# Context, norm and queries of the first layer in one block, with the mask counted instead of kept

## What is computed

```
n = layernorm(x);  q = n @ wq.T + bq;  k = ctx @ wk.T + bk;  v = ctx @ wv.T + bv     (16 heads of 16)
scores = q k^T / 4;  scores = -inf where mask == 0;  a = softmax(scores) v;  y = a @ wo.T + bo
x = x + tanh(g_xattn) * y;  then a gated mixture of experts on layernorm(x)
```

## Time and profile before

| | us |
|---|---|
| median of 3 runs | 1854.36 (1853.82 to 1856.44) |
| the profiled execution | 1838.9 |
| its span, first to last instruction | 1837.2 |
| busy: PE, DVE, ACT, POOL | 1497.6, 1178.2, 860.9, 180.8 |
| mean granted TensorE clock | 0.903 |

### The profile page before, as it was taken

The page is one execution under the profiler, slowest core; times in us unless marked ns, Lnnn a source line. Parts: engine busy times, 40 slices in busy tenths (PEclk is TensorE's granted clock), DMA queues, the critical chain, the costliest instruction groups (busy, mean ns, idle before and its releaser), DMA issues. The chain is left out here.

```text
span 1837.2 us, 23827 instructions
## 1 busy us (share of the span) xinstructions
PE 1497.6 (82%) x7833; PEld 871.9 (47%) x7834; DVE 1178.2 (64%) x2309; ACT 860.9 (47%) x1544; POOL 180.8 (10%) x248
## 2 busy tenths in 40 slices
PE   6564999968997899992399999999999987848870
PEld 3232333347886788882153334333334334735550
DVE  2564999763311677776299999999999935502335
ACT  3121777722111555550217777777777773211110
POOL 3520000000300000003000000000000000061116
PEclk9786999987999999996759999999999998778995
DMA  7935422112101899981723112112111100533114
GB/s 240 373 104 170 119 54 54 28 48 69 46 0 68 321 333 340 343 290 60 217 58 81 43 29 40 23 24 45 24 23 25 23 1 1 125 107 114 43 43 137
DMA packets 108667, 196.87 MB, mean 107 GB/s; under 512 B 8959, under 2 KB 80372, under 8 KB 108568
## 3 DMA queue, kind: packets, MB, share of 16 engines
q1 hardware_dynamic: 101633, 180.71, 31.4%
q0 software_dynamic: 4608, 12.59, 2.2%
q10 hardware_dynamic: 2326, 2.31, 0.4%
HBM read 144.69 MB, written 50.36 MB: 106 GB/s over the span
## 5 line engine op out<-in xcount | busy, mean ns | idle before, releaser
L920 DVE TENSOR_REDUCE attend_piece_max<-attend_p_bank 128x1 f32<-128x400 f32 (+3 forms) x1280 | 669.2, 589 | 68.8 <-PE attend_p_bank L808 56.5
L900 ACT ACTIVATE attend_probs<-attend_s_bank 128x512 f32<-128x512 f32 (+1 forms) x1088 | 565.7, 602 | 244.0 <-PE attend_s_bank L819 244.0
L808 PE MATMUL attend_p_bank<-attend_k_st,attend_q_st 62*128 62x400 f32 (+2 forms) x1280 | 416.6, 435 | 55.3 <-DMA attend_k_st<-ones_rows 50.8
L819 PE MATMUL attend_s_bank<-attend_q_st,attend_k_st 64*128 64x512 f32 (+1 forms) x1088 | 402.4, 448 | 36.6 <-ACT attend_probs L900 21.7
L819 PEld LDWEIGHTS attend_s_bank<-attend_q_st,attend_k_st 64*128 64x128 f32 (+1 forms) x1088 | 172.2, 183 | 359.0 <-ACT attend_probs L900 351.6
L836 PE MATMUL attend_o_bank<-attend_probs,attend_v_st 128*32 128x512 f32 (+1 forms) x2176 | 291.0, 607 | 1.4 <-ACT attend_probs L900 1.4
L808 PEld LDWEIGHTS attend_p_bank<-attend_k_st,attend_q_st 62*128 62x128 f32 x1280 | 209.2, 194 | 104.0 <-issue 52.5
L1530 DVE TENSOR_TENSOR slots_w_low<-slots_w_up,slots_w_high 128x2048 fp32r<-128x2048 f32 x46 | 105.1, 2287 | 45.7 <-ACT slots_w_high L1526 45.7
L1340 DVE TENSOR_TENSOR share_hid<-share_b_bank,share_g_act 128x512 f32<-128x512 f32 (+1 forms) x40 | 27.6, 691 | 116.7 <-PE share_b_bank L1191 105.5
L1526 ACT ACTIVATE slots_w_high<-slots_w_up 128x2048 fp32r<-128x2048 f32 x46 | 87.8, 1910 | 5.8 <-DMA slots_w_up<-in_L_ffn_W_dram 5.6
L1797 POOL DMA_INDIRECT collect_back<-back,keep_f_place x48 | 47.1, 982 | 381.1 <-PEq L1786 367.1
(11 more groups left out here) (234 smaller groups left out, 1810.1 us busy)
## 6 DMA issues: line engine op xcount, KB each, us to landing
slots_w_up<-in_L_ffn_W_dram SPq DMA_DIRECT2D x46, 1024.0 KB, 7.4
slots_w_dn<-in_L_ffn_W_dram SPq DMA_DIRECT2D x23, 1024.0 KB, 5.9
ctx_raw<-in_mask_BxSxS_ik_dram SPq DMA_DIRECT2D x16, 800.5 KB, 8.2
q_rows<-q_part SPq DMA_DIRECT2D x24, 512.0 KB, 4.0
attend_q_st<-q_rows SPq DMA_DIRECT2D x64, 192.0 KB, 4.6
k_rows<-ctx_k_part SPq DMA_DIRECT2D x12, 800.5 KB, 10.0
attend_k_st<-k_rows SPq DMA_DIRECT2D x32, 300.2 KB, 5.8
sorted<-keep_zeros SPq DMA_DIRECT2D x6, 1024.0 KB, 9.7
```

Source lines behind the costliest of these rows:

```text
L808: last = pe.matmul(bank[:, 0:even(kn)], q_st[rows, slot, t * P:(t + 1) * P].bitcast(F32R), k_st[rows, slot, k0:k0 + even(kn)].bitcast(F32R ...
L819: last = pe.matmul(out, k_st[rows, hs, kt * P:kt * P + kn].bitcast(F32R), q_st[rows, hs, q0:q0 + CH].bitcast(F32R), start=True, stop=not m ...
L900: act.activation(probs[0:kn, (kt + hs) % RING, q0:q0 + CH], s_bank[(NC * kt + c + hs) % RING][0:kn, :], ACT.Exp).then_inc(exp_done, 1)
L920: dve.tensor_reduce(dst, bank_of(i, n)[:, 0:kn], AX.X, ALU.max).then_inc(entry_done, 1)
```

## The change

One block, `prepare`, takes the place of `prepare_context`, `normalise` and `project_queries` for the first layer; the second layer keeps the latter two.

- x is loaded ahead of the mask, in four parts; the statistics are taken behind the context's copies, and the norm and the queries come between the first layer's keys and the values. The second layer's keys come last.
- ACT writes keys and queries once, rounded; DVE computes the low part from PSUM, (bank + bias) - rounded, piece by piece. `k_full` and `full` are gone. Keys have a ring of three units, queries a ring of three halves, values a ring of four, PSUM two rings of four and three banks. The query weights are scaled when they are copied.
- The mask tiles have a ring of four. They aren't converted and kept: DVE adds (tile == 0) onto one bf16 tile for 12 of them, with one instruction each, and POOL onto another for 4 (tiles 3, 7, 11, 15), with two. PE's column sums take both. `find_ends` compares counts and not sums of -2^100. In the branch on all keys, the mask is loaded and converted there (`load_mask` as a function).
- `find_ends`, `find_window` and the store of `key_mask` move into the block, and their small operations with them.

The diff, cut to its core:

```diff
--- before.py
+++ after.py
...
-def prepare_context(nc, io, const, scratch, mask_q, unseen, x_now, stats):
+def prepare(nc, io, const, scratch, unseen, x_now, window):
...
-        names = [f"L{l}_xattn_w{w}" for w in order for l in range(2)]
-        NW, WR, LOADS, VR = len(names), 4, 4, 2
+        sc = Scope(nc, ctx, "prep")
+        names = [f"L{l}_xattn_w{w}" for w, l in ("k0", "q0", "v0", "v1", "k1", "q1", "o0", "o1")]
+        NW, WR, LOADS, VR, RR, KR, QR, XR = len(names), 4, 4, 4, 4, 3, 3, 4
...
-        k_full = sc.sb("k_full", [P, DB, S], F32)
-        k_part = sc.sb("k_part", [P, PART, DB, S], F32)
+        q_bias = sc.sb("q_bias", [P, DB], F32)
+        k_part = sc.sb("k_part", [P, KR, PART, S], F32)
+        q_part = sc.sb("q_part", [P, QR, PART, HALF], F32)
...
+        raw = sc.sb("raw", [P, RR, S], I32)
+        masked = [sc.sb(f"masked_{n}", [P, S], BF16) for n in ("dve", "pool")]
...
+        a_bank = [sc.ps(f"a_bank{n}", [P, CH], F32) for n in range(4)]
+        b_bank = [sc.ps(f"b_bank{n}", [P, CH], F32) for n in range(3)]
...
+            for n, t in enumerate(on_pool):
+                pool.wait_ge(landed[t % RR], 16 * (t // RR + 1))
+                pool.wait_ge(counted[1], n + 1)
+                pool.tensor_scalar(flag[:, :], raw[:, t % RR], 0.0, None, ALU.is_equal).then_inc(flagged, 1)
+                pool.wait_ge(flagged, n + 1)
+                pool.tensor_tensor(masked[1][:, :], masked[1][:, :], flag[:, :], ALU.add).then_inc(counted[1], 1)
...
-            load_mask(0)
-            load_mask(1)
-            for n, (l, b) in enumerate(units):
-                for t in range(2 + AHEAD * n, 2 + AHEAD * (n + 1)):
-                    load_mask(t)
...
+            for n in range(2):
+                load_weights(n)
+            for n in range(4):
+                sp.dma_start(x_now[:, 4 * n:4 * n + 4], io["x"][0].rearrange("(t p) d -> p t d", p=P)[:, 4 * n:4 * n + 4])\
+                    .then_inc(x_in[n], 16)
+            for t in range(RR):
+                load_mask(t)
+            for n in range(2, WR):
+                load_weights(n)
+            store_keys(0)
+            load_mask(4)
+            store_keys(1)
+            for t in range(5, 9):
+                load_mask(t)
+            for n in range(4):
+                store_queries(n)
+                load_mask(9 + n)
+            for n in range(WR, NW):
+                load_weights(n)
+            for t in range(13, QT):
+                load_mask(t)
+            for kt in range(KT):
+                store_values(kt)
+            for u in (2, 3):
+                store_keys(u)
...
-            pe.wait_ge(copied, 4)
+            pe.wait_ge(w_copied, 1)
             pe.wait_ge(c_copied, KT)
...
+            for u in range(DB):
+                for c in range(NP):
+                    keys(u, c)
+            for n in range(QT // 2):
+                bank = take(1, b_bank, x_copied, n + 1)
+                for t in (2 * n, 2 * n + 1):
+                    pe.wait_ge(scaled, t + 1)
...
+            pe.wait_ge(w_copied, 2)
+            for n, (b, c) in enumerate(q_tiles):
+                bank = take(0, a_bank, q_low, n + 1)
+                pe.wait_ge(x_copied, 2 * (c + 1))
...
+            for n in range(2, WR):
+                turn_weight(n)
+            pe.wait_ge(w_copied, WR)
             for kt in range(KT):
-                if kt >= 2:
-                    pe.wait_ge(v_added, kt - 1)
+                bank = take(1, b_bank, v_added, kt + 1)
...
-            pe.wait_ge(k_copied, 2 * len(chunks))
-            for n in range(4, NW):
+            for n in range(WR, NW):
...
-            pe.wait_ge(merged, QT)
+            pe.wait_ge(counted[0], len(on_dve) + 1)
+            pe.wait_ge(counted[1], len(on_pool) + 1)
             for kt in range(KT):
                 kn = keys_of(kt)
-                pe.matmul(unseen[0:kn, kt:kt + 1], tile_sum[:, kt * P:kt * P + kn], ones[:, :], start=True, stop=True)
+                for n in range(2):
+                    last = pe.matmul(unseen[0:kn, kt:kt + 1], masked[n][:, kt * P:kt * P + kn], ones[:, :],
+                                     start=(n == 0), stop=(n == 1))
+            last.then_inc(scored, 1)
+            for u in (2, 3):
+                for c in range(NP):
+                    pe.wait_ge(w_copied, WR + 1)
+                    keys(u, c)
...
+            act.wait_ge(stable, 1)
+            act.activation(std[:, :], var[:, :], ACT.Sqrt).then_inc(rooted, 1)
+            for u in range(DB):
+                round_keys(u)
...
+            for n, (b, c) in enumerate(q_tiles):
+                act.wait_ge(q_ready, n + 1)
+                if n // 2 >= QR:
+                    act.wait_ge(q_stored[n // 2 - QR], 16 * PRODUCTS)
+                act.activation(q_part[:, n // 2 % QR, 0, c % 2 * CH:(c % 2 + 1) * CH].bitcast(F32R), a_of("q", n)[:, :],
+                               ACT.Identity, bias=q_bias[:, b:b + 1]).then_inc(q_high, 1)
+            for n in range(2, NW):
                 copy_weight(n)
+            for u in (2, 3):
+                round_keys(u)
...
+            left = list(on_dve)
+
+            def count_masks(n):
+                for t in left[:n]:
+                    dve.wait_ge(landed[t % RR], 16 * (t // RR + 1))
+                    dve.wait_ge(counted[0], on_dve.index(t) + 1)
+                    dve.scalar_tensor_tensor(out=masked[0][:, :], in0=raw[:, t % RR], scalar=0.0, in1=masked[0][:, :],
+                                             op0=ALU.is_equal, op1=ALU.add).then_inc(counted[0], 1)
+                del left[:n]
...
+            def split_keys(u):
+                l, b = units[u]
+                if u >= KR:
+                    dve.wait_ge(k_stored[u - KR], 16 * PRODUCTS)
+                for c, (k0, kn) in enumerate(PIECES):
+                    n = NP * u + c
+                    dve.wait_ge(k_high, n + 1)
+                    dve.scalar_tensor_tensor(out=k_part[:, u % KR, 1, k0:k0 + kn].bitcast(F32R),
+                                             in0=a_of("k", n)[:, 0:kn],
+                                             scalar=const["bqk"][:, (2 * l + 1) * DB + b:(2 * l + 1) * DB + b + 1],
+                                             in1=k_part[:, u % KR, 0, k0:k0 + kn], op0=ALU.add, op1=ALU.subtract)\
+                        .then_inc(k_low, 1)
...
+            for t in range(QT):
+                dve.wait_ge(x_in[t // 4], 16)
+                dve.bn_stats(stats[:, t], x_now[:, t]).then_inc(measured, 1)
...
+            dve.tensor_scalar(var[:, :], mv[:, :, 1], 1e-5, None, ALU.add).then_inc(stable, 1)
+            dve.wait_ge(b_copied, 1)
+            split_keys(0)
+            dve.wait_ge(rooted, 1)
+            dve.reciprocal(inv[:, :], std[:, :]).then_inc(inverted, 1)
+            count_masks(1)
+            split_keys(1)
+            dve.wait_ge(inverted, 1)
+            for t in range(QT):
+                if t >= XR:
+                    dve.wait_ge(x_turned, (t - XR) // 2 + 1)
+                dve.tensor_scalar(x_n[:, t % XR], x_now[:, t], mv[:, t, 0:1], inv[:, t:t + 1], ALU.subtract, ALU.mult)\
+                    .then_inc(scaled, 1)
+            dve.wait_ge(bias_ready, 1)
+            for n, (b, c) in enumerate(q_tiles):
+                dve.wait_ge(q_high, n + 1)
...
+                dve.scalar_tensor_tensor(out=q_part[:, n // 2 % QR, 1, at].bitcast(F32R), in0=a_of("q", n)[:, :],
+                                         scalar=q_bias[:, b:b + 1], in1=q_part[:, n // 2 % QR, 0, at], op0=ALU.add,
+                                         op1=ALU.subtract).then_inc(q_low, 1)
+                if n % 2 == 0:
+                    count_masks(1)
             dve.wait_ge(bv_in, 64)
             for kt in range(KT):
                 kn = keys_of(kt)
                 dve.wait_ge(v_ready, kt + 1)
                 if kt >= VR:
                     dve.wait_ge(v_stored[kt % VR], 16 * (kt // VR))
-                dve.tensor_tensor(v_out[0:kn, kt % VR].rearrange("p l d -> p (l d)"), bank[2 + kt % 2][0:kn, :],
+                dve.tensor_tensor(v_out[0:kn, kt % VR].rearrange("p l d -> p (l d)"), b_of("v", kt)[0:kn, :],
                                   bv[0:kn].rearrange("p l d -> p (l d)"), ALU.add).then_inc(v_added, 1)
-                if AHEAD * len(units) + kt < QT:
-                    convert(AHEAD * len(units) + kt)
-            dve.wait_ge(x_in, 16)
+                count_masks(1)
+            count_masks(len(left))
+            find_ends(dve, unseen, key, score, hidden[:, :], touched[:, :], ends, numbered, scored)
+            split_keys(2)
+            split_keys(3)
+            dve.wait_ge(ends_turned, 1)
+            dve.tensor_copy(hidden_row[:, :], unseen[0:KT, P:2 * P]).then_inc(row_copied, 1)
+            find_window(dve, turned_ends, choice, window, ends_turned, stepped)
...
-    everywhere, anywhere = NEG * (T - 0.5), NEG * 0.5
+    everywhere, anywhere = T - 0.5, 0.5
+    dve.wait_ge(scored, 1)
...
```

(85 more changed lines are left out.)

247 lines of the change are left out of this document (138 added, 109 removed).

## The result

| | changed | before |
|---|---|---|
| median, first comparison (4 runs each) | 1840.8 us (1838.55 to 1842.48) | 1854.09 us (1853.46 to 1856.44) |
| median, second comparison | 1823.99 us | 1842.46 us |
| median, third comparison | 1824.92 us | 1841.76 us |

The ratio of the first is 0.992 (0.9908 to 0.9932): faster by 13.3 us, where 13 had been forecast, with 1841.4 us as the time. The two repeats, on other chips, give 0.9899 (0.9884 to 0.9914) and 0.9913 (0.9897 to 0.9928), 18.5 and 16.8 us. The range, 1826 to 1862 us, was laid around a time before of 1854.36 us and stands for anything from 28 us less to 8 us more; all three differences are inside it.

A forecast was written before the change was run, and what follows sets the result against it. It saw a transfer-bound first part, then a compute-bound second. The new timeline ran to 138 us, plus 4 made 142 against 155: 13 us off the 1854.36 us median, 1841.4 us, range 1826 to 1862.

The forecast's parts named there:

- both waits: ACT about 9 us at about 52 for a query store; DVE about 20 us near 76 for the first value store.
- Start to first keys: Block's start: context's last copy at 21.1, keys start at 23.4, variances at 27.8, first key unit done at 30.8.
- Count, unit 1, norm: After the first keys: count 1.8 us, second key unit done at 35.5, 16 scalings 5.3 us, x copied at 42.
- Queries: After the norm: 1.75 us per tile, six done at 52.5, then a store wait landing at 62; values start at 65.
- Values: After queries: four added at 76, wait to 97, POOL's comparison of 2 to 6 us hidden there, nine tiles to 112.
- Weights, sums, second keys, stores: Block's end: four weights 3.8 us, sums to 117, second layer's keys 11 us to 128, last store landed at 138.
- Borders: Block borders: two vanish, their time already in the difference because ends are compared.
- The lump of 4 us: Added to 138 at the end: DVE two-input operations held once or twice by POOL, and some queries or keys at lower clock.
- B: Rival, chance 0.20: transfers pack better, value stores come sooner, end of the stretch at 128, time 1827 us.
- C: Rival, chance 0.15: gain eaten on DVE, five two-input operations held by POOL cost 14 us; 1855, no change.
- D: Rival, chance 0.15: PE at the lower clock after stalls, 31 us more, end at 169, 1868 us, slower.
- The frame: Change touches only what runs up to 157 us; some 1680 us behind stay, and over 3 us change there disproves it.

The follow-up runs named there:

- the pair on one chip: Changed kernel and kernel before, both without edit, profiled in the third comparison: ratio 0.9913, POOL's first memset of the attention at 145.94 and 158.43 us.
- the earlier trace: Profiled execution of the kernel before, without edit, from which the prediction took its prices: 1838.9 us.
- the experiment without POOL: Changed kernel with all 16 mask tiles counted by DVE and none by POOL: 1817.87 us, ratio 0.9867, memset 136.99.
- two rings: Changed kernel with a fourth half for queries and values 4 to 11 in x_nt's space: 1805.1 us, ratio 0.98, memset 127.11.

## Why the prediction came out right, step by step

The difference was right to 0.3 us in the first comparison and 5.5 and 3.8 us short in the repeats. At the memset, where all 13 us were forecast, it was 11.5 us between the first profiles and 12.5 in the pair on one chip; the rest came from behind it, where nothing was forecast. The path held, as did both waits and their places. But the steps' times were too early nearly throughout, and the 4 us added at the end happened to cover it: the last landing, forecast at 138 and at 142 with them, came at 143.5. That much of the hit is luck.

1. *Start to first keys.* "I take the same time: its last copy ends at 21.1" failed: the context's last copy ended at about 18.0, 3.1 us sooner, and first keys started at 19.6 and not 23.4. Beside x the context comes faster than beside the mask: with x behind four masks the last copy ended at 24.4. x itself came later than the 20 that I had named, DVE waiting for it until 21.3 in this profile. The variances were ready at 25.5 (27.8). The low part is 0.63 us (0.57).
2. *Count, unit 1, norm.* The count alone is 1.77 to 1.82 us, as taken; its mean is 2.17 with the held ones. Unit 1 was done at 34.0 (35.5). "16 scalings of 0.33 us" failed: 10.22 and not 5.3 us, for the two instructions that POOL held. "0.33 us each" was right only without POOL: 5.7 and 5.25 us for all 16 in two runs where POOL is idle then. The forecast had priced POOL's contention only against two-input operations, and put it at the end as a lump. x was copied at 45.3 (42).
3. *Queries.* Eight tiles took 13.9 us at the full clock, 1.74 each, as in the earlier trace rows. The wait was there: until 67.4 (62), 11.8 us long (9). Of these 5.4 us, 3.1 are the store's later issue, at 56.9 (53.8), which follows from x's late copy; the other 2.3 it took longer to land, behind four masks.
4. *Values.* Four were added at 81.3 (76); the wait was 19.4 us (20) and ended at 103.6 (97), with a share of 1.0 to 1.04 from 80 to 100 us. "Between 2 and 6 us it hides in this wait" is the step that failed: POOL's comparison takes 4.27 us, inside its bounds, but it does not hide. Mask 15 could be issued only after it and the addition, 7.5 us in all, and the value stores stood behind mask 15. Behind the wait, nine tiles took 18.1 us and not 15: two counts were held by POOL (3.63 and 4.23), 4.2 us together.
5. *Weights, sums, second keys, stores.* Four weights took 1.91 us, half of the 3.83 of the earlier trace rows, at a granted clock of 1.00 by the profile in both places. The pace casts doubt on that for the early one: this kernel's first weights (8 transposes in 1.97 us at 17.7) go at 0.21 us from one start to the next, much as x's do at a granted clock of 0.50 (30 in 6.22 us, 0.20 each), and the late ones at 0.11. So the price that I took from the earlier trace rows looks like one of the lower level, though no run tested it. The second keys ran from 123.3 to 134.3, 11.0 us as forecast, 6 us late; the six stores were issued from 129.6 to 137.1, and the last landed at about 143.5, two before the memset as in the earlier trace rows. Memset 145.7, against 144.
6. *Borders.* Nothing showed there.
7. *The lump of 4 us.* In kind it was right (DVE held by POOL: 4.9 in step 2, some 4 in step 4), and it was too small.

**Rivals.** B (transfers pack better, memset 130) did not happen, but its reason was sound: freed of the two waits, the kernel does just that. C's mechanism is real and cost about 7 us, not 14, which the experiment without POOL shows; with 7 in place of the 4 added, the forecast would have been 3 us further from what was measured and better in reasoning. D did not happen: second keys and queries ran at 1.00. Its reasoning held for short pieces behind a stall: 30 transposes of x at a clock of 0.57 (38 to 45 us), and four value instructions that, behind the long wait, took 3.78 us at a clock of 0.50 and the next 2.13.
The Trainium skill (TensorE: Matmul & The Clock Gate, What's actually happening) has the clock come back once PE is kept busy; the trace agrees with that pair of durations.

**The frame.** "If the part behind 157 us changes by more than 3 us, the frame of the sum is wrong": between the first two profiles it grew by 14.9 us (1680.1 to 1695.0). The two are not of one occasion: the profile of before, 1838.9 us, is 15 us below its own three runs, while that of the changed kernel, 1842.48 us, is one of the four that make its median. The loss lies in the shared experts of both layers, whose code is untouched; there ACT stood in three places, 23.7 us in all, for something that the profile doesn't name:

```profile
ACT share_g_act L1413 <- remote: 23.7, 3, 12.3
```

None of the other 13 profiles has this row, ten of them with the changed block, so it is not the change. It may well be what made that occasion slow: all four runs of the changed kernel there are over 13 us above the medians of the repeats (1838.55 us at least, against 1823.99 and 1824.92), and 14.9 us would be most of it. Before ran 12 us longer there too, but no profile of it was taken then, and what ACT waited for is open.

In the other profiles of the changed block the part behind is 1676.8 to 1680.7 us (ten), in those of before 1680.1 to 1683.0 (three): some 3 us on average in its favour, and 5.8 us in the pair on one chip. By my own line of 3 us the frame is therefore not quite sound: a few microseconds of the repeats' gain are not in the stretch that the sum describes. No single place carries them, and why is open.

## What to carry to other kernels

When a store is queued behind loads, and the loads behind the buffers that another engine has yet to free, every engine in that chain is on the path, however idle it looks: price GpSimd's work as if it weren't hidden until you have followed the queue. Give moved work its own buffers before looking for a faster instruction: two rings brought 19 us where the whole change brought 17. And work taken off VectorE onto GpSimd can lengthen both; here giving it back was worth 7 us.

## What was unexpected of the hardware

- A one-input fp32 scaling of 0.41 us stood 3.37 us while POOL ran one addition of 3.21 us; the loss comes in whole instructions of POOL's, not as a rate.
- POOL's comparison of 128 x 1601 int32 takes 4.27 us, where DVE does comparison and addition in 1.8 us. Its last addition, beside DVE's held counts, took 3.67 us and not 3.21.
- The profile shows a granted clock of 1.00 for the first 20 us, while the transposes there follow each other at 0.21 us, the pace of a granted 0.50; late in the block it is 0.11.
- Each of the two kernels differs by 12 to 17 us between occasions, while the difference of the two stays within 13 to 19: a comparison needs both on the same chip.
